# A selective-scan kernel: four states turned and three multiplied by GpSimd instead of three and four, their last columns kept by ScalarE, and the chunk loops written out

## The chip, the cores and the metric

One core of one Trainium2 chip. The metric is the device time of one execution in microseconds (us). The engines are TensorE (PE; PEld is its weight load), VectorE (DVE), ScalarE (ACT), GpSimd (POOL) and SyncE (SP), which here issues nearly all DMAs. Each engine runs its own list of instructions in order and waits on semaphores.

## The reference, cut to what matters

The input x is 2 x 4096 x 512. A layer norm with a modulation goes before two Mamba blocks, one forward and one backward in time; their outputs are projected, gated and added to x, and then a small quantized linear layer follows. The part that takes the time is the scan over 4096 positions, with 1024 channels and 16 states for each channel:

```
dA  = exp(delta[..., None] * A)
dBu = (delta * u)[..., None] * Bm[:, :, None, :]
def step(h, t):
    dA_t, dBu_t, C_t = t
    h = dA_t * h + dBu_t
    return (h, einsum('bdn,bn->bd', h, C_t))
y = (ys + u * Dp) * silu(z)
return y @ wout.T
```

## The kernel before, in words

There are three stages: a setup, the scan stage, which this change touches, and a final stage for the linear layer. The scan stage works through 32 chunks of 512 time steps (16 forward, 16 backward). A chunk has 8 tiles `j` of 128 channels, and a tile has 8 positions `q` of two states each, `n = 2q` and `2q + 1`; `p = 8j + q` counts the positions of a chunk, and `g` counts tiles over all chunks.

For every state of every tile:

- ACT computes dA = exp(delta * A) into one of four places (`step_dA`, L796 to L807; `PLACES = 4`). So dA of state n can be made only once state n - 4 no longer needs its place: for a straight state when DVE has multiplied it (`hC_made`), for the others when its scan is done (`h_made`).
- POOL computes dBu for two states at once (L692).
- DVE runs the scan h = dA * h + dBu (L1153).

Then the state is multiplied by C and summed over the 16 states. This is done in three ways:

- Nine straight states: DVE multiplies (L1169), and PE adds the product, transposed, into the bank `yT` (`add_state`, L1013 to L1018).
- `ASIDE`, four states (3, 4, 7, 11): the scan writes `hR`, POOL multiplies it in place (L701) at position `JOINS[n]`, three positions after the scan at most, and PE adds it there.
- `TURNED`, three states (1, 5, 9): the scan writes `hV`. PE transposes it into the one PSUM bank `OWN_BANK` (event `T`, `transpose_state`, L990) at position n // 2 + 1. ACT then takes it out at position `TAKE`, multiplying by C, which after the transpose is one number for each partition: four activations of 128 x 128 (`take_turned`, L769 to L775). At the start of the next tile PE adds these transposed pieces back (event `Y`, `turn_back`, L1020 to L1032), and DVE multiplies the result by the gate z (`gate`, L1121) at position 1.

The last column of each scan is the start of the same tile's scan in the next chunk. DVE copies it to `state`: straight states at L1165 and L1174, `hR` and `hV` states at L1183.

The rest of the network runs beside this as a background schedule (`SCHEDULE`): each event (Z and U: projections of four pairs of matmuls; O: output projection of eight; C: convolution; D: step; X, K, H: others) has positions at which PE issues its pieces, ahead of that position's additions to `yT`, and a `TAKE` position at which ACT empties its bank. A bank is written again only after it was taken (`bank_free`). Within a position PE goes by the first position of the event, and at equal first positions by Y, D, Z, T, others. So an O event that began earlier comes ahead of T.

Once a tile, at the positions in `GATED` (the last position of tiles 0 to 5 and 7, position 4 of tile 6), ACT loads the table for silu, runs one or two silus, and loads the table for exp again (L909 to L915). The order of ACT at a position is: dA of state 2q, then the `MIDWAY` takes (`Z` of this tile and the last `T` of a tile), dA of state 2q + 1, then the other takes, then the gated part. The lines that the steps of the prediction touch:

```
TAKE = {name: at[-1] + (2 if name[0] in "ZTUCDXK" else 1) ...}      # L101
PER_TILE += [(f"T{j*N+n}", (j*NQ + n//2 + 1,), OWN_BANK) ... for n in TURNED]   # L84
```

With TURNED = (1, 5, 9) the T events are at positions 1, 3 and 5 of a tile, and ACT takes them at 3, 5 and 7. The outer loops of ACT, PE, POOL and DVE are `Fori` loops of 4 rounds with 8 chunks written out in each.

Of the kernel before, what the change touches and what calls it, by code (L numbers as in the profile page):

```python
# [13 lines left out]
P = 128  # L14
D = 512
# [28 lines left out]
TURNED = (1, 5, 9)  # L44
ASIDE = (3, 4, 7, 11)
# [5 lines left out]
COPIES = ((3, 4), (7,), (11,))  # L51
# [3 lines left out]
HC, HR, HV = 4, 4, 3  # L55

TURN = 8
# [43 lines left out]
TAKE = {name: at[-1] + (2 if name[0] in "ZTUCDXK" else 1) for name, at, bank in SCHEDULE}  # L101
# [258 lines left out]
def scan_stage(nc, io, dram):  # L360

    with ExitStack() as ctx:
# [80 lines left out]
        def _(sp):  # L443
# [212 lines left out]
        def _(pool):  # L656
# [24 lines left out]
            with pool.Fori(0, CHUNKS // TURN) as r:  # L681
                for v in range(TURN):
                    i, s = r * TURN + v, v % 2
                    for j in range(MT):
                        g = i * MT + j
                        pool.wait_ge(du_made, g + 1)
                        for q in range(NQ):
                            p = j * NQ + q
                            pool.wait_ge(h_made, g * N + 2 * (q + 1 - AHEAD) + H0)
                            if j == 0:  # L690
                                pool.wait_ge(B_loaded[q], i * 16 + 16)
                            pool.tensor_tensor(dBu[:, q % AHEAD], Bb[:, 2 * q:2 * q + 2, :],  # L692
                                               du[:, j % 2, :].unsqueeze(1).broadcast_to([P, 2, T]),
                                               ALU.mult).then_inc(dBu_made, 1)
                            for n in ASIDE:
                                if q == JOINS[n]:
                                    k = ASIDE.index(n)
                                    pool.wait_ge(aside_saved, copied(g, n) + A0)
                                    if j == 0:
                                        pool.wait_ge(C_loaded[n // 2], i * 16 + 16)  # L700
                                    pool.tensor_tensor(hR[:, k, :], hR[:, k, :], Cb[:, n, :], ALU.mult).then_inc(hR_made, 1)  # L701
                            if q == 6:
                                m, ms = (j + 1, s) if j + 1 < MT else (0, 1 - s)
                                pool.wait_ge(dA_made, g * N + DU0)
                                pool.wait_ge(dBu_made, g * NQ + 1)
                                steps(g + 1, m, ms, i * MT + 2 * MT)

        @block.scalar
        def _(act):
            def take_step(made, bank, g, m):  # L710

                act.wait_ge(bg_ready, made)
                if not isinstance(g, int) or g > 0:
                    act.wait_ge(delta_made, g)
# [16 lines left out]
            def take_u(made, bank, c, m, stored):  # L731
                act.wait_ge(bg_ready, made)
                if m < 2 and not isinstance(c, int):
                    act.wait_ge(out_stored[m], c * 32 + O0)
                act.wait_ge(hist_stored, stored)
                if not isinstance(c, int) or m >= 2:
# [60 lines left out]
            def step_dA(g, j, v, n):  # L797
# [6 lines left out]
                else:  # L804
                    act.wait_ge(h_made, tile * N + before + 1 + H0)
                act.activation(place(n)[:], delta[:, j % 2, :], ACT.Exp,  # L806
                               scale=A[:, v % 2, j * N + n:j * N + n + 1]).then_inc(dA_made, 1)  # L807
# [36 lines left out]
            with act.Fori(0, CHUNKS // TURN) as r:  # L844
                for v in range(TURN):
                    i, s = r * TURN + v, v % 2
                    bank = lambda name: bg[BANK[name]]
                    act.wait_ge(bg_free, freed(i - 1, "K"))
                    act.wait_ge(A_loaded[s], r * (8 * TURN) + (v // 2 * 16 + 16))
# [778 lines left out]
```

## Time and profile before

| | |
|---|---|
| median of 3 runs | 7603.56 us (7603.14 to 7606.13) |
| profiled execution | 7600.66 us, of which the span is 7598.7 us |
| busy, share of the span | PE 90%, DVE 92%, POOL 92%, ACT 80% |
| granted TensorE clock, mean | 0.973 |
| costliest groups | POOL dBu (L692) 4788 us, DVE scans (L1153) 5165 us in three groups, ACT dA (L806) 2746 us, DVE products (L1169) 1557 us |

The first scan is at 225 us, the last at about 7160 us; nearly all of the rest is setup and final stage. How to read it: three engines are busy nine tenths of the span, so the shares alone don't say which one sets the time. The idle times ahead of each engine's instructions, and what ended them, do. A record of a DVE or ACT instruction reaches some 0.1 us into the next one's, so the time that an instruction really costs is the distance from its start to the next start.

### The profile page before, as it was taken

The page shows a single profiled execution, that of the slowest core. Times are in us where ns is not written, and L with a number is a line of the kernel's source. Part 1 is how long each engine was busy: PE and PEld are TensorE (multiplying, and loading weights), DVE is VectorE, ACT ScalarE, POOL GpSimd, SP SyncE. Part 2 cuts the span into 40 slices and gives each one's busy share as a digit, 9 for nine tenths or more (in the row PEclk, how much of TensorE's full clock was granted, in tenths as well). Part 3 has the DMA queues.
Part 4 walks back from the last instruction along what each step waited for, and adds up shares of the span by engine and source line. Part 5 has one row for each costly group of instructions (what it writes and reads, how often), then busy time and mean ns, then how long its engine had stood idle before and what let it go on. Part 6 is the DMA issues. An engine that isn't in the chain of part 4 may idle for free. (4 is left out here: it accounts for less than half of the span.)

```text
span 7598.7 us, 137446 instructions
## 1 busy us (share of the span) xinstructions
PE 6830.6 (90%) x32682; PEld 4035.6 (53%) x32682; DVE 6955.4 (92%) x10093; ACT 6069.6 (80%) x11545; POOL 6968.9 (92%) x3774
## 2 busy tenths in 40 slices
PE   6899999899898989999898999999898999999889
PEld 3455555555555555555555555555555555555455
DVE  2799999999999999999999999999999999999766
ACT  1788888888788888888788888888788888888645
POOL 0899999999999999999999999999999999999678
PEclk8999999999999999999999999999999999999999
DMA  8444445444444454444445544444355444444555
GB/s 258 145 137 134 128 139 149 128 120 144 132 134 126 141 150 124 123 143 138 122 129 145 149 113 136 139 137 134 117 150 149 107 141 135 138 130 131 152 193 172
DMA packets 605609, 1066.02 MB, mean 140 GB/s; under 512 B 113584, under 2 KB 221872, under 8 KB 596336
## 3 DMA queue, kind: packets, MB, share of 16 engines
q1 hardware_dynamic: 602704, 1055.84, 46.9%
q8 instruction: 289, 4.73, 0.3%
q14 instruction: 536, 4.39, 0.2%
q10 hardware_dynamic: 2080, 1.05, 0.0%
HBM read 926.61 MB, written 130.05 MB: 139 GB/s over the span
## 5 line engine op out<-in xcount | busy, mean ns | idle before, releaser
L692 POOL TENSOR_TENSOR dBu<-Bb,du 128x1024 f32<-128x1024 f32 x2048 | 4787.8, 2365 | 74.9 <-DVE hV L1153 44.2
L1153 DVE TENSOR_TENSOR_SCAN scans<-scans,state,dBu 128x512 f32<-128x512 f32 x2304 | 2902.8, 1280 | 393.6 <-ACT scans L806 363.1
L806 ACT ACTIVATE scans<-delta,A 128x512 f32<-128x512 f32 x4096 | 2745.7, 691 | 557.4 <-DVE hC L1169 480.9
L1016 PE MATMUL yT<-ident,hC 128*128 128x128 f32 x9216 | 1407.4, 282 | 344.1 <-DVE hC L1169 340.8
L1169 DVE TENSOR_TENSOR hC<-scans,Cb 128x512 f32<-128x512 f32 x2304 | 1556.8, 680 | 12.2 <-PE yT L1016 12.2
L1016 PEld LDWEIGHTS yT<-ident,hC 128*128 128x128 f32 x9216 | 1058.6, 143 | 774.8 <-DVE hC L1169 536.4
L701 POOL TENSOR_TENSOR hR<-hR,Cb 128x512 f32<-128x512 f32 x1024 | 1290.0, 1270 | 190.2 <-DVE state L1183 183.7
L1153 DVE TENSOR_TENSOR_SCAN hR<-scans,state,dBu 128x512 f32<-128x512 f32 x1024 | 1293.4, 1263 | 0.5
L1009 PE MATMUL bg<-u,comb 128*128 128x512 f32 x2112 | 989.1, 594 | 0.9 <-DVE u L1125 0.9
L1153 DVE TENSOR_TENSOR_SCAN hV<-scans,state,dBu 128x512 f32<-128x512 f32 x768 | 968.6, 1261 | 13.1 <-ACT scans L806 12.8
L948 PE MATMUL bg<-hT,win_u 128*128 128x512 f32 x2112 | 966.5, 598 | 0.9 <-ACT hT L728 0.9
L970 PE MATMUL bg<-hT,win_z 128*128 128x512 f32 x2048 | 963.3, 593 | 0.0
L773 ACT ACTIVATE turned<-bg,CT 128x128 f32<-128x128 f32 x3072 | 863.1, 363 | 14.4 <-PE bg L993 12.8
L1016 PEld LDWEIGHTS yT<-ident,hR 128*128 128x128 f32 x4096 | 493.1, 148 | 282.9 <-issue 254.7
L1016 PE MATMUL yT<-ident,hR 128*128 128x128 f32 x4096 | 620.9, 287 | 0.0
L948 PEld LDWEIGHTS bg<-hT,win_u 128*128 128x128 f32 x2112 | 382.3, 191 | 444.0 <-issue 437.7
L993 PEld LDWEIGHTS bg<-ident,hV 128*128 128x128 f32 x3072 | 369.2, 142 | 433.5 <-issue 257.6
L993 PE MATMUL bg<-ident,hV 128*128 128x128 f32 x3072 | 471.7, 276 | 90.0 <-ACT turned L773 59.8
L1009 PEld LDWEIGHTS bg<-u,comb 128*128 128x128 f32 x2112 | 368.6, 190 | 330.9 <-issue 329.2
L970 PEld LDWEIGHTS bg<-hT,win_z 128*128 128x128 f32 x2048 | 359.2, 190 | 306.0 <-issue 306.0
L963 PE MATMUL bg<-comb,wtap 128*32 128x512 f32 x2080 | 292.7, 636 | 212.1 <-DMA comb<-pre_scratch 207.1
L1027 PEld LDWEIGHTS bg<-ident,turned 128*128 128x128 f32 x3084 | 379.8, 149 | 155.5 <-issue 155.5
(163 smaller groups left out, 7586.9 us busy)
## 6 DMA issues: line engine op xcount, KB each, us to landing
comb<-pre_scratch SPq DMA_DIRECT2D x1040, 256.0 KB, 4.6
Bb<-bc_scratch SPq DMA_DIRECT2D x264, 512.0 KB, 8.6
Cb<-bc_scratch SPq DMA_DIRECT2D x264, 512.0 KB, 7.9
win_u<-in_win SPq DMA_DIRECT2D x264, 256.0 KB, 4.9
pre_scratch<-pre SPq DMA_DIRECT2D x264, 256.0 KB, 3.7
comb<-comb_scratch SPq DMA_DIRECT2D x66, 1024.0 KB, 8.0
win_z<-in_win SPq DMA_DIRECT2D x257, 256.0 KB, 2.7
part_scratch<-pre SPq DMA_DIRECT2D x132, 256.0 KB, 2.0
```

Source lines behind the costliest of these rows:

```text
L692: pool.tensor_tensor(dBu[:, q % AHEAD], Bb[:, 2 * q:2 * q + 2, :], du[:, j % 2, :].unsqueeze(1).broadcast_to([P, 2, T]), ALU.mult).then_in ...
L701: pool.tensor_tensor(hR[:, k, :], hR[:, k, :], Cb[:, n, :], ALU.mult).then_inc(hR_made, 1)
L773: ins = act.mul(turned[:, TURNED.index(n), tt * P:(tt + 1) * P], bank[:, tt * P:(tt + 1) * P], CT[:, s, tt, n:n + 1])
L806: act.activation(place(n)[:], delta[:, j % 2, :], ACT.Exp, scale=A[:, v % 2, j * N + n:j * N + n + 1]).then_inc(dA_made, 1)
L948: ins = nc.tensor.matmul(bank[:], win_u[:, m % RING, k, :], hT[:, slot, k, :], start=(k == 0), stop=(k == KD - 1))
L970: ins = nc.tensor.matmul(bank[:], win_z[:, j % 2, k, :], hT[:, slot, k, :], start=(k == 0), stop=(k == KD - 1))
L993: ins = nc.tensor.matmul(bank[:, tt * P:(tt + 1) * P], hV[:, TURNED.index(n), tt * P:(tt + 1) * P], ident[:], start=True, stop=True, is_tr ...
L1009: ins = nc.tensor.matmul(bank[:], comb[:, m, tt * P:(tt + 1) * P], u[:, s, m, :], start=(k == 0), stop=(k == MT - 1))
L1016: ins = nc.tensor.matmul(yT[:, tt * P:(tt + 1) * P], product[:, tt * P:(tt + 1) * P], ident[:], start=first and tt == 0, stop=False, is_tr ...
L1027: nc.tensor.matmul(bank[:, tt * P:(tt + 1) * P], turned[:, k, tt * P:(tt + 1) * P], ident[:], start=False, stop=False, is_transpose=True, ...
L1153: nc.vector.tensor_tensor_scan(to, place(n)[:], dBu[:, q % AHEAD, k, :], state[:, c:c + 1], ALU.mult, ALU.add).then_inc(h_made, 1)
L1169: nc.vector.tensor_tensor(hC[:, (j * NS + STRAIGHT.index(n)) % HC, :], bank[:], Cb[:, n, :], ALU.mult).then_inc(hC_made, 1)
```

## The change

1. `TURNED` becomes (2, 5, 8, 11) and `ASIDE` (1, 4, 7). The nine straight states are now 0, 3, 6, 9, 10, 12, 13, 14, 15. POOL multiplies three states a tile instead of four (at positions 3, 5 and 6); PE transposes four instead of three and adds four back.
2. T events are now at positions 2, 3, 5 and 6 of a tile, and ACT takes a turned state at the next position (3, 4, 6, 7), not at the one after that. The last of them is still taken midway in position 7.
3. The last columns of the turned and aside states are copied by ACT (`keep_states`), four positions of states later, not by DVE.
4. The `Fori` loops of ACT, PE, POOL and DVE are written out over all 32 chunks.
5. SP waits for `hR_used` (PE has added) instead of `hR_made` (POOL has multiplied) before it loads C again.

```
-TURNED = (1, 5, 9)
-ASIDE = (3, 4, 7, 11)
+TURNED = (2, 5, 8, 11)
+ASIDE = (1, 4, 7)
-COPIES = ((3, 4), (7,), (11,))
+COPIES = ((1,), (4,), (7,))
-HC, HR, HV = 4, 4, 3
+HC, HR, HV = 4, NA, NT
-TAKE = {name: at[-1] + (2 if name[0] in "ZTUCDXK" else 1) for name, at, bank in SCHEDULE}
+TAKE = {name: at[-1] + (2 if name[0] in "ZUCDXK" else 1) for name, at, bank in SCHEDULE}
...
-                            sp.wait_ge(hR_made, aside(last, 2 * q + 2))
+                            sp.wait_ge(hR_used, aside(last, 2 * q + 2) + R0)
...
-            with pool.Fori(0, CHUNKS // TURN) as r:
-                for v in range(TURN):
-                    i, s = r * TURN + v, v % 2
+            for i in range(CHUNKS):
+                s = i % 2
...
+            def keep_states(g, j, n):
+
+                for ns, places, saved in [(ns, hR, aside_saved) for ns in COPIES] + [(TURNED, hV, turned_saved)]:
+                    if n != ns[-1] + 4:
+                        continue
+                    act.wait_ge(h_made, g * N + ns[-1] + 1 + H0)
+                    k = (ASIDE if places is hR else TURNED).index(ns[0])
+                    step = ns[1] - ns[0] if len(ns) > 1 else 1
+                    act.copy(state[:, j * N + ns[0]:j * N + ns[-1] + 1:step],
+                             places[:, k:k + len(ns), T - 1]).then_inc(saved, 1)
...
+                        step_dA(g, i, j, 2 * q)
+                        keep_states(g, j, 2 * q)
...
+                        step_dA(g, i, j, 2 * q + 1)
+                        keep_states(g, j, 2 * q + 1)
...
-                            for n in pair:
-                                for ns, places, saved in [(ns, hR, aside_saved) for ns in COPIES] + [(TURNED, hV, turned_saved)]:
-                                    if n != ns[-1]:
-                                        continue
-                                    dve.wait_ge(h_made, g * N + n + 1 + H0)
-                                    k = (ASIDE if places is hR else TURNED).index(ns[0])
-                                    step = ns[1] - ns[0] if len(ns) > 1 else 1
-                                    nc.vector.tensor_copy(state[:, j * N + ns[0]:j * N + n + 1:step],
-                                                          places[:, k:k + len(ns), T - 1]).then_inc(saved, 1)
```

## Rows read from the trace of the kernel before

**Rows 1.** Waits over the whole span: who waited for whom, us in total, times, longest.

```profile
ACT scans L806 <- DVE hC L1169: 480.9, 465, 9.5
DVE scans L1153 <- ACT scans L806: 363.1, 195, 119.9
POOL hR L701 <- DVE state L1183: 183.7, 228, 1.5
DVE scans L1153 <- issue: 29.9, 3, 10.3
ACT turned L773 <- PE bg L993: 12.8, 30, 0.9
```

**Rows 2.** Groups of instructions by line and shape: busy us, mean ns of one, idle before.

```profile
L701 POOL TENSOR_TENSOR hR<-hR,Cb 128x512 f32<-128x512 f32 x1024 | 1290.0, 1270 | 190.2 <-DVE state L1183 183.7
L1183 DVE COPY state<-hV 128x3 f32<-128x3 f32 x256 | 89.5, 350 | 0.0
L1183 DVE COPY state<-hR 128x2 f32<-128x2 f32 x256 | 79.2, 309 | 0.0
L1183 DVE COPY state<-hR 128x1 f32<-128x1 f32 x512 | 73.6, 144 | 0.0
L874 ACT ACTIVATE state<-state,cur 128x16 f32<-128x16 f32 x256 | 75.6, 295 | 0.0
```

**Rows 3.** Busy time by tile of chunk 12: window, length, PE, PEld, DVE, ACT, POOL, clock, DMA.

```profile
2852.90:2879.90 27.00, 27.00 (x127) 16.59 (x128) 26.30 (x38) 20.64 (x40) 26.82 (x16) 1.00 0.10 33
...
sum 214.46, PE 196.48 PEld 116.96 DVE 207.68 ACT 182.00 POOL 208.25; mean PE 24.56 PEld 14.62 DVE 25.96 ACT 22.75 POOL 26.03
```

**Rows 4.** Timeline of PE in tile 1 (2852.90 to 2879.90): start us, us, instruction.

```profile
2861.06 0.60 PE L1016 MATMUL yT<-ident,hC 128*128 128x128 f32 x4
2861.49 1.88 PE L1009 MATMUL bg<-u,comb 128*128 128x512 f32 x4
2863.21 1.88 PE L970 MATMUL bg<-hT,win_z 128*128 128x512 f32 x4
2864.93 0.60 PE L993 MATMUL bg<-ident,hV 128*128 128x128 f32 x4
...
2872.71 0.60 PE L1016 MATMUL yT<-ident,hC 128*128 128x128 f32 x4
```

**Rows 5.** Timeline of ACT in the same tile.

```profile
2861.40 1.12 ACT L773 ACTIVATE turned<-bg,CT 128x128 f32<-128x128 f32 x4
...
2875.14 0.78 ACT L782 ACTIVATE pre<-bg,gain 128x512 f32<-128x512 f32 x1 [0.87 <-PE bg L1009]
2875.94 1.28 ACT L909 ACT_TABLE_LOAD   x1
...
2879.18 1.91 ACT L806 ACTIVATE scans<-delta,A 128x512 f32<-128x512 f32 x3
```

**Rows 6.** Timeline of DVE in the same tile: scans of states 6, 8, and the next tile.

```profile
2861.89 0.85 DVE L1183 COPY state<-hR 128x2 f32<-128x2 f32 x1
2862.65 1.28 DVE L1153 TENSOR_TENSOR_SCAN scans<-scans,state,dBu 128x512 f32<-128x512 f32 x1
...
2865.67 0.14 DVE L1183 COPY state<-hR 128x1 f32<-128x1 f32 x1
2865.73 1.28 DVE L1153 TENSOR_TENSOR_SCAN scans<-scans,state,dBu 128x512 f32<-128x512 f32 x1
...
2879.90 1.29 DVE L1153 TENSOR_TENSOR_SCAN scans<-scans,state,dBu 128x512 f32<-128x512 f32 x1 [0.71 <-ACT scans L806]
```

**Rows 7.** Timeline of PE and ACT at the end of tile 3 (2906.56 to 2933.04).

```profile
2925.09 0.60 PE L993 MATMUL bg<-ident,hV 128*128 128x128 f32 x4
...
2926.40 0.60 PE L1016 MATMUL yT<-ident,hC 128*128 128x128 f32 x4
...
2928.13 1.28 ACT L909 ACT_TABLE_LOAD   x1
...
2932.31 1.92 ACT L806 ACTIVATE scans<-delta,A 128x512 f32<-128x512 f32 x3
```

More of the change, by code:

```diff
@@ L712, in take_step @@
                 act.wait_ge(bg_ready, made)
-                if not isinstance(g, int) or g > 0:
+                if g > 0:
                     act.wait_ge(delta_made, g)
@@ L944, in project_u @@
                 pe.wait_ge(wu_loaded[m % RING], (c * per + m // RING + 1) * 16)
-                if m == 0 and not isinstance(c, int):
+                if m == 0 and c > 0:
                     pe.wait_ge(bg_free, freed(c - 2, "H3"))
@@ new lines, in _ @@
+            for i in range(CHUNKS):
+                s = i % 2
+                for j in range(MT):
+                    g = i * MT + j
+                    dve.wait_ge(state_kept, g - 6 + K0)
+                    for q in range(NQ):
+                        p = j * NQ + q
+                        dve.wait_ge(state_saved, kept(g, q) + S0)
+                        dve.wait_ge(dBu_made, g * NQ + q + 1)
+                        for k in range(2):
+                            n = 2 * q + k
+                            c = j * N + n
+                            dve.wait_ge(dA_made, g * N + n + 1 + DU0)
+                            if n in ASIDE:
+                                dve.wait_ge(hR_used, aside(g, n) + 1)
+                                to = hR[:, ASIDE.index(n), :]
+                            elif n in TURNED:
+                                dve.wait_ge(bg_ready, ready(i if j else i - 1, f"T{((j - 1) % MT) * N + n}"))
+                                dve.wait_ge(turned_saved, g + V0)
+                                to = hV[:, TURNED.index(n), :]
+                            else:
+                                to = place(n)[:]
+                            nc.vector.tensor_tensor_scan(to, place(n)[:], dBu[:, q % AHEAD, k, :],
+                                                         state[:, c:c + 1], ALU.mult, ALU.add).then_inc(h_made, 1)
+                        if q == 1:
+                            name = f"Y{(j - 1) % MT}"
+                            gate(ready(i, name), bg[OWN_BANK], g - 1, (j - 1) % MT, s if j else 1 - s)
+                        pair = (2 * q, 2 * q + 1)
+                        own = [n for n in pair if n in STRAIGHT]
+                        for n in own:
+                            c = j * N + n
+                            dve.wait_ge(h_made, g * N + n + 1 + H0)
+                            bank = place(n)
+                            if len(own) == 1:
+                                nc.vector.tensor_copy(state[:, c:c + 1], bank[:, T - 1:T]).then_inc(state_saved, 1)
+                            dve.wait_ge(hC_used, straight(g, n) - C0 + 1)
+                            if j == 0 and n == own[0]:
+                                dve.wait_ge(C_loaded[q], i * 16 + 16)
+                            nc.vector.tensor_tensor(hC[:, (j * NS + STRAIGHT.index(n)) % HC, :], bank[:],
+                                                    Cb[:, n, :], ALU.mult).then_inc(hC_made, 1)
+                            if n == pair[0]:
+                                dve.wait_ge(h_made, g * N + n + 2 + H0)
+                            if n == pair[0] and len(own) == 2:
+                                nc.vector.tensor_copy(state[:, c:c + 2],
+                                                      scans[:, n % PLACES:n % PLACES + 2, T - 1]).then_inc(state_saved, 1)
```

275 lines of the change are left out of this document (112 added, 163 removed).

## The prediction

> **What bounds the kernel now.** I read the waits first, then the groups of instructions, then one chunk tile by tile, and last the timeline of two tiles.
>
> The busy shares name three candidates, POOL, DVE and PE, each near nine tenths. The waits separate them [rows 1]. DVE's scans wait for dA of ACT: 363.1 us in total, of which 119.9 us is the one wait ahead of the first scan, so about 243 us fall within the scan stage. DVE has no wait of this size for POOL. POOL in turn waits 183.7 us for DVE's copies. So POOL, though as busy as DVE, is not what the scans wait for. ACT is the least busy of the four, but it works in order and waits 480.9 us for DVE's products, because it has only four places for dA. The picture: DVE sets the pace, and where ACT is held up in one place for long, DVE stops.
>
> Rows 3 show it for chunk 12, 214.46 us long: DVE is busy 207.68 us of it, POOL 208.25, PE 196.48, ACT 182.00. In tile 1 PE is busy 27.00 us of 27.00: there PE has no slack at all. Most tiles end with a stop of DVE for dA of the next tile's first state, as at 2879.90, 0.71 us [rows 6]: just before, ACT did its two table loads and silu.
>
> **What goes away.**
>
> POOL's fourth multiply: 256 x 1.27 us = 325 us of POOL's busy time [rows 2]. I count it at nothing, since no scan waits for POOL [rows 1]. At most it could be worth what POOL costs elsewhere.
>
> By the Trainium skill, GPSIMD Engine Reference, sections 1 (Specifications) and 2 (Architecture), GpSimd shares its SBUF port with VectorE, which contends with it in instructions with two SBUF inputs. If DVE stood still for all of the removed 325 us, the time would be 7603.6 - 325 = 7279. The trace speaks against it: DVE's scans take 1.28 to 1.29 us wherever they stand beside POOL's work [rows 6].
>
> DVE's copies for `hR` and `hV`: four a tile. Their busy times sum to 89.5 + 79.2 + 73.6 = 242 us [rows 2], but records overlap. From start to next start the one-column copy costs 0.06 us (2865.67 to 2865.73) and the slow two-column one 0.76 us (2861.89 to 2862.65) [rows 6]. Bounds: 256 x 4 x 0.06 = 61 us, and 242 us. I take about 90 us of DVE time. It is worth that only in tiles where DVE itself is the last; where DVE waits for ACT it is worth nothing.
>
> The loops: three waits of about 10 us, 29.9 us in all, that no engine ended [rows 1]; they are the three jumps back of the four-round loops. Written out they go: -30 us. The other waits are then on constants instead of registers. What a hand-over costs is seen at 2879.18: dA of 0.65 us, and the scan that waits for it starts at 2879.90 [rows 5, 6], so at most 0.1 us could go. Two such hand-overs a tile would be 51 us; I count 0 and keep the 51 us of gain as the bound.
>
> **What is added.** ACT gets four more activations a tile for the fourth turned state. Four of them cost 1.0 us from the first to the next instruction's start (the block of 1.12 us includes the tail) [rows 5], so 256 us. It also gets four small copies a tile; the nearest row is its 128x16 multiply, 295 ns [rows 2], whose real cost lies between 0.1 and 0.3 us; 0.2 x 4 x 256 = 205 us. PE gets one transpose group and one turn-back group more, one addition less: +4 matmuls of 128x128 a tile at 0.44 us a group [rows 4]. ACT's 182 us a chunk become about 196 of 214: it still fits on average. Averages don't decide here; order does.
>
> **The order.** Before, a turned state had two positions between PE's transpose and ACT's take, and ACT waited only 12.8 us in all for it [rows 1]. A position lasts 3.1 us or more (2862.65 to 2865.73) [rows 6]. Now it has one position. ACT reaches the take one position (over 3 us) earlier, while PE's transpose of the same position comes no earlier. So ACT will wait, and what stands behind the take on ACT is dA of states 2q + 2 and on, and at a tile's end the table loads, silu, and dA of the next tile's first state. DVE waits for those. I work out two tiles.
>
> Tile 1, middle. Now the second turned state (2) is transposed at position 2. PE's addition for position 1 stood at 2861.06; it moves up 0.44 us, as T of position 1 is gone, and ends about 2861.06. Ahead of T at position 2 come the two pieces of O1 (1.72 us) and of Z1 (1.72 us), then T with its tail, 0.60: ready at 2865.1 [rows 4]. ACT began its take in the same position 3 at 2861.40 [rows 5]; now it begins at 2865.1, ends it 1.0 us later, and makes dA of state 8 in 0.65: 2866.8, where DVE wants it at 2865.73 [rows 6]. DVE stops for 1.1 us.
>
> Tile 1, end. PE's own chain: T of position 3 waits for the bank until 2866.2, 1.3 us later than its 2864.93; the turn-back has 0.44 more. So the addition of state 10 moves from 2872.71 to about 2874.4 and ends at 2874.9. At position 6 the two O2 pieces come first (1.72), then the new T of state 11: ready about 2877.1. ACT takes it midway in position 7: 1.0, then dA of state 15, 0.65, the copy of four columns, 0.2, O2's take, 0.8: 2879.75. From the table load to dA of the next tile it is 3.24 us (2875.94 to 2879.18), and that dA takes 0.7 [rows 5]: the next tile starts at 2883.7, not 2879.90, less the 0.1 us by which PE's chain closes up: +3.7 us.
>
> Tile 3, end (no O pieces at position 6). PE's addition of state 10 ends about 2926.4, and T of state 11 is ready at 2927.0 [rows 7]. But ACT must first take state 8 (transposed at position 5, where a transpose stood at 2925.09: ready at 2925.7), 1.0, then dA of state 14, 0.65: 2927.35. Take, dA 15, copy and U3's take (as O2's): 1.0 + 0.65 + 0.2 + 0.8: 2930.0. Table load to dA is 4.18 us here, with two silus (2928.13 to 2932.31), plus 0.7: 2934.9 against 2933.04, +1.8 us.
>
> The other tiles by the same steps in the same views, by what stands ahead of T: tile 2 has O3 and Z2 pieces ahead of T of state 2 and U0, U1 (3.4 us each) at positions 4 and 5: +3.8. Tile 5 has the convolution C6 at position 5, which waits for a DMA: +3.8. Tile 6 has its table loads at position 4, and the take of state 5 now stands ahead of them with its 1.0 us, after a late one of state 2: +2.6. Tile 4 has U4 at position 1: +1.6; tile 7 +1.4; tile 0, with the least ahead of T, +0.9. These are estimates of mine from the timelines of PE and ACT, of which rows 4, 5 and 7 stand for two tiles.
>
> **The sum.** A chunk: 0.9 + 3.7 + 3.8 + 1.8 + 1.6 + 3.8 + 2.6 + 1.4 = 19.6 us, 9% of 214.46. Times 32: +627 us. The copies taken from DVE give nothing in it, as every tile now ends with a wait for ACT. Loops: -30. Profiled execution 7600.7 + 627 - 30 = 8198; the median lies 3 above the profiled one: 8200 us, rounded.
>
> Other places: SP now waits for PE's addition before it reloads C, so the loads of B behind it in SP's queue come later by a few us once a chunk. POOL needs B of the next chunk two positions or more later, and chunks get longer: 0, with 2 us x 32 = 64 as the bound above.
>
> **Rivals.**
>
> 1. Less of it. Only the tile ends count, and PE is never behind. Then state 11's T comes right after the addition of state 10, as in tile 3, and the middle of tiles costs nothing: 6 to 12 us a chunk. 7600.7 - 30 + 192 to 384 = 7760 to 7955. For it: ACT has up to three states of lead, and a longer tile gives PE time to catch up. Against: PE is full in tile 1 [rows 3], and what stands ahead of T is PE's own work.
>
> 2. Faster. T is ready when ACT comes, so the order costs nothing, and DVE's copies and the loops are gained: 7603.6 - 30 - 61 = 7512, down to 7603.6 - 30 - 242 = 7332 by the busy times. It decides at one point: whether PE has T of state 11 ready when ACT has made dA of state 14. For it: ACT is idle a fifth of a chunk [rows 3]. Against: that idle time is waiting for DVE's products [rows 1], and the table loads come after the take.
>
> 3. POOL runs dry. POOL's multiply of state 4 at position 5 now waits for ACT's copy, which comes behind dA of state 8; in tile 1 that is 2867.0, and POOL still has multiplies of 1.23 each, dBu of 2.3 each and the steps, about 10.7 us, before dBu of the last position, which the scan wants at 2876.7. It is late by 1 us there, in the three heavy tiles: 3 x 32 x 1.1 = +106 us, 8306, and more only if POOL's lateness carried from tile to tile.
>
> 4. No change: rival 1's lower half meets rival 2's gains, 7590 to 7615.
>
> **How the numbers follow.** The forecast (8000 to 8400: a third of the 627 less, or rival 3 and the 64 us of the loads more) has 0.55, rival 1 0.27, rival 2 0.10, the port rule 0.01, rival 4 0.04, rival 3 above 8400 0.03. Likeliest: 8200 us. The range reaches from 7680 to 8400: below it are the cases of faster and no change (0.15), above it 0.03. A measurement of this kernel tells 0.2% (15 us) from no change. Faster 0.11, within 0.2% 0.04, slower 0.85.
>
> **What would show each step.** ACT's turned group waits for PE's transposes by hundreds of us instead of 12.8. DVE's scans wait for ACT's dA by over 700 us instead of 243 in the stage, at a tile's first state and at state 8. The wait "issue" of 29.9 us is gone. POOL's busy time falls by about 325 us and its idle time grows by more. Tiles 1, 2 and 5 are over 30 us long. The prediction is wrong if ACT's takes find T ready as before, or if the scans' waits for ACT don't grow.

## The result and the profile after

The median is 8305.32 us (8303.13 to 8310.12, 4 runs) against 7603.35 us for the kernel before in the same set: the ratio is 1.0925, interval 1.0911 to 1.0939, so 702 us slower. The profiled execution took 8304.09 us, its span is 8302.3 us and the mean granted clock 0.958, against 0.973.

Part 1 of the page of the kernel after (busy us, share of the span, instructions):

```profile
PE 7105.6 (86%) x33710; PEld 4219.8 (51%) x33710; DVE 6887.6 (83%) x9069; ACT 6412.4 (77%) x13593; POOL 6662.7 (80%) x3518
```

No engine is above 86% now. GpSimd, relieved of a quarter of its multiplies, and VectorE, relieved of its copies, both stand idle a sixth of the time or more. Where they stand is in the waits. These are the waits of the kernel after that answer to [rows 1] (who waited for whom, us in total, times, longest):

```profile
POOL hR L698 <- ACT state L814: 1270.1, 639, 6.7
ACT turned L770 <- PE bg L1002: 966.7, 576, 4.7
DVE scans L1160 <- ACT scans L803: 888.8, 479, 119.9
DVE hV L1160 <- PE bg L1002: 179.9, 128, 2.4
PE bg L1002 <- ACT turned L770: 162.0, 192, 1.2
ACT scans L803 <- DVE hC L1176: 82.0, 128, 1.3
DVE hV L1160 <- ACT scans L803: 74.3, 93, 1.6
DVE scans L1160 <- issue: 24.9, 124, 0.2
```

ACT's take waits 966.7 us for PE's transpose, where it waited 12.8 us before. The scans wait 888.8 us for dA; less the 119.9 us ahead of the first scan that is 769 us, against 243. Another 254 us are lost ahead of the scans that write `hV`, all of them at state 8. Summed by state over the 256 tiles, without the wait ahead of the very first scan, the scans' stops are 443 us at state 0, 254 at state 8, 178 at state 10, 144 at state 15 and 31 at state 14; in the kernel before they are 178 (30 of them the jumps of the loops), 16, 79, 0 and 0. ACT's waits for VectorE's products have shrunk from 480.9 to 82.0 us: ACT no longer runs ahead of VectorE, it runs behind. The three waits of 10 us are gone (no "issue" wait of a scan is over 0.2 us).

Three groups of the kernel after, to be set beside [rows 2] (busy us, mean ns | idle before):

```profile
L698 POOL TENSOR_TENSOR hR<-hR,Cb 128x512 f32<-128x512 f32 x768 | 977.6, 1273 | 1270.5 <-ACT state L814 1270.1
L770 ACT ACTIVATE turned<-bg,CT 128x128 f32<-128x128 f32 x4096 | 1175.7, 380 | 975.4 <-PE bg L1002 966.7
L814 ACT COPY state<-hR 128x1 f32<-128x1 f32 x768 | 155.4, 202 | 0.0
```

Chunk 12 by tile, the windows of the kernel after, from first scan to first scan (columns as in [rows 3]):

```profile
3093.23:3120.88 27.65, 27.01 (x118) 15.73 (x117) 25.86 (x33) 22.09 (x48) 24.79 (x14) 0.95 0.56 222
3120.88:3151.44 30.56, 29.08 (x139) 17.84 (x138) 25.68 (x34) 22.74 (x49) 27.05 (x15) 1.00 0.09 29
3151.44:3181.74 30.30, 27.77 (x130) 16.71 (x128) 25.86 (x34) 23.14 (x52) 24.52 (x14) 1.00 0.46 126
3181.74:3211.00 29.26, 25.88 (x141) 14.76 (x140) 25.64 (x33) 24.65 (x54) 25.28 (x14) 1.00 0.55 137
3211.00:3239.63 28.63, 23.93 (x121) 13.32 (x119) 25.56 (x34) 24.73 (x54) 23.26 (x14) 1.00 0.61 148
3239.63:3270.66 31.03, 26.39 (x145) 16.14 (x143) 25.67 (x34) 25.26 (x55) 27.78 (x15) 1.00 0.45 106
3270.66:3304.48 33.82, 23.32 (x97) 11.65 (x96) 25.77 (x33) 26.89 (x55) 22.88 (x13) 0.89 0.18 53
3304.48:3332.04 27.56, 22.20 (x123) 16.73 (x122) 25.64 (x35) 23.26 (x51) 23.12 (x14) 0.87 0.58 186
```

VectorE is busy about 25.7 us in every tile, however long the tile is: all that was added is standing still. The chunk is 238.8 us long against 214.46 [rows 3]. The lengths of the same tiles of the kernel before, from first scan to first scan, give the growth:

| tile | 0 | 1 | 2 | 3 | 4 | 5 | 6 | 7 |
|---|---|---|---|---|---|---|---|---|
| before, us | 26.3 | 27.0 | 26.7 | 26.5 | 26.8 | 27.7 | 28.1 | 25.5 |
| after, us | 27.7 | 30.6 | 30.3 | 29.3 | 28.6 | 31.0 | 33.8 | 27.6 |
| growth | 1.4 | 3.6 | 3.6 | 2.8 | 1.8 | 3.4 | 5.8 | 2.1 |
| growth, mean of all chunks | 1.5 | 3.5 | 3.6 | 2.5 | 1.8 | 2.8 | 5.4 | 1.8 |
| forecast | 0.9 | 3.7 | 3.8 | 1.8 | 1.6 | 3.8 | 2.6 | 1.4 |

The fourth line is the same difference in the mean of the 32 chunks, without the three jumps. Chunk 12 is not typical in one tile: before the change its tile 5 took 27.7 us, where the mean of that tile is 29.0.

### The profile page after: what moved, and what is told of

It is laid out like the page before. It is cut to its first block and busy times, and to the rows that moved or that the text cites. A ratio compares the mean times of both kernels' runs of the same rounds, so it can differ in the third digit from the quotient of the medians.

```text
span 8302.3 us, 112807 instructions
## 1 busy us (share of the span) xinstructions
PE 7105.6 (86%) x33710; PEld 4219.8 (51%) x33710; DVE 6887.6 (83%) x9069; ACT 6412.4 (77%) x13593; POOL 6662.7 (80%) x3518
## 5 line engine op out<-in xcount | busy, mean ns | idle before, releaser
L1160 DVE TENSOR_TENSOR_SCAN scans<-scans,state,dBu 128x512 f32<-128x512 f32 x2304 | 2908.9, 1278 | 923.0 <-ACT scans L803 888.8
L698 POOL TENSOR_TENSOR hR<-hR,Cb 128x512 f32<-128x512 f32 x768 | 977.6, 1273 | 1270.5 <-ACT state L814 1270.1
L770 ACT ACTIVATE turned<-bg,CT 128x128 f32<-128x128 f32 x4096 | 1175.7, 380 | 975.4 <-PE bg L1002 966.7
L1160 DVE TENSOR_TENSOR_SCAN hV<-scans,state,dBu 128x512 f32<-128x512 f32 x1024 | 1298.8, 1268 | 254.3 <-PE bg L1002 179.9
L1160 DVE TENSOR_TENSOR_SCAN hR<-scans,state,dBu 128x512 f32<-128x512 f32 x768 | 970.6, 1264 | 0.0
L1002 PE MATMUL bg<-ident,hV 128*128 128x128 f32 x4096 | 651.1, 283 | 162.0 <-ACT turned L770 162.0
L1002 PEld LDWEIGHTS bg<-ident,hV 128*128 128x128 f32 x4096 | 496.1, 144 | 561.3 <-issue 315.3
L1036 PEld LDWEIGHTS bg<-ident,turned 128*128 128x128 f32 x4112 | 501.8, 149 | 183.1 <-issue 183.1
L1036 PE MATMUL bg<-ident,turned 128*128 128x128 f32 x4112 | 519.9, 282 | 0.0
L1025 PE MATMUL yT<-ident,hR 128*128 128x128 f32 x3072 | 481.0, 280 | 0.0
L1025 PEld LDWEIGHTS yT<-ident,hR 128*128 128x128 f32 x3072 | 374.5, 146 | 149.1 <-issue 149.1
```

Source lines behind the costliest of these rows:

```text
L770: ins = act.mul(turned[:, TURNED.index(n), tt * P:(tt + 1) * P], bank[:, tt * P:(tt + 1) * P], CT[:, s, tt, n:n + 1])
L1002: ins = nc.tensor.matmul(bank[:, tt * P:(tt + 1) * P], hV[:, TURNED.index(n), tt * P:(tt + 1) * P], ident[:], start=True, stop=True, is_tr ...
L1025: ins = nc.tensor.matmul(yT[:, tt * P:(tt + 1) * P], product[:, tt * P:(tt + 1) * P], ident[:], start=first and tt == 0, stop=False, is_tr ...
L1036: nc.tensor.matmul(bank[:, tt * P:(tt + 1) * P], turned[:, k, tt * P:(tt + 1) * P], ident[:], start=False, stop=False, is_transpose=True, ...
L1160: nc.vector.tensor_tensor_scan(to, place(n)[:], dBu[:, q % AHEAD, k, :], state[:, c:c + 1], ALU.mult, ALU.add).then_inc(h_made, 1)
```

## Inside two tiles

**Tile 1**, for which the prediction worked out every step. From the timelines of PE, ACT and DVE of the kernel after, put in order of time (start us, us, instruction, in brackets the idle time before it):

```profile
3132.39 0.60 PE L1002 MATMUL bg<-ident,hV 128*128 128x128 f32 x4
3133.02 1.14 ACT L770 ACTIVATE turned<-bg,CT 128x128 f32<-128x128 f32 x4 [1.38 <-PE bg L1002]
3134.04 0.71 ACT L803 ACTIVATE scans<-delta,A 128x512 f32<-128x512 f32 x1
3135.04 1.28 DVE L1160 TENSOR_TENSOR_SCAN hV<-scans,state,dBu 128x512 f32<-128x512 f32 x1 [2.08 <-PE bg L1002]
...
3144.21 0.60 PE L1002 MATMUL bg<-ident,hV 128*128 128x128 f32 x4
3144.84 1.14 ACT L770 ACTIVATE turned<-bg,CT 128x128 f32<-128x128 f32 x4 [1.31 <-PE bg L1002]
...
3151.44 1.29 DVE L1160 TENSOR_TENSOR_SCAN scans<-scans,state,dBu 128x512 f32<-128x512 f32 x1 [2.30 <-ACT scans L803]
```

The tile starts at 3120.88. The transpose of state 2 is ready 12.1 us into it (forecast 2865.1 - 2852.90 = 12.2), the one of state 11 at 23.9 (forecast 24.2), and the tile is 3.6 us longer (forecast 3.7). The stop in the middle is 2.08 us, where 1.1 was forecast. The scan of state 8 starts 14.2 us into the tile (forecast 13.9), so most of the difference seems to be on the other side: VectorE had done its product 12.1 us into the tile and not 12.8, as the slow two-column copy of [rows 6] is no longer ahead of it. What the copy gave back is stood still here, one instruction on. (The profile names PE as the releaser, since this scan waits for several semaphores; the transpose in question is that of the tile before and was long done. Of what the scan needs, dA came last: it was begun at 3134.04, behind the take, and ended 0.29 us before the scan; dBu had ended 5 us before it.)

**Tile 6**, where the forecast was worst. The timelines of PE and DVE of the kernel after, in order of time:

```profile
3286.90 1.93 PE L988 MATMUL bg<-u,wx 128*64 128x512 f32 x4
3288.76 0.65 PE L1002 MATMUL bg<-ident,hV 128*128 128x128 f32 x4
...
3291.31 1.29 DVE L1160 TENSOR_TENSOR_SCAN scans<-scans,state,dBu 128x512 f32<-128x512 f32 x1 [5.05 <-ACT scans L803]
...
3294.47 1.11 PE L1025 MATMUL yT<-ident,hC 128*128 128x128 f32 x4 [4.62 <-DVE hC L1176]
3295.51 3.68 PE L988 MATMUL bg<-u,wx 128*64 128x512 f32 x4
3299.12 1.12 PE L1002 MATMUL bg<-ident,hV 128*128 128x128 f32 x4
...
3302.03 1.29 DVE L1160 TENSOR_TENSOR_SCAN scans<-scans,state,dBu 128x512 f32<-128x512 f32 x1 [2.53 <-ACT scans L803]
```

And the windows of the same stretch (the number ahead of the DMA share is the granted clock):

```profile
3285.00:3290.00 5.00, 3.82 (x19) 1.78 (x17) 1.23 (x3) 4.95 (x8) 1.47 (x1) 1.00 0.00 0
3290.00:3292.50 2.50, 0.00 (x0) 0.00 (x0) 1.19 (x1) 2.49 (x6) 0.52 (x1) 1.00 0.00 0
...
3295.00:3297.50 2.50, 2.50 (x6) 0.92 (x5) 2.50 (x5) 0.64 (x2) 2.50 (x2) 0.50 0.00 0
3297.50:3300.00 2.50, 2.50 (x6) 0.89 (x6) 1.82 (x2) 0.00 (x0) 2.50 (x2) 0.50 0.04 7
```

The first stop, at state 10, is the one that was forecast: ACT does its table loads and silus at position 4, now with the take of state 5 ahead of them. It is 5.05 us, where the kernel before stopped 2.44 us: 2.6 us more, exactly the term of the sum. What the sum did not have is the second stop, 2.53 us at state 15. While VectorE stood, PE had nothing to add and was idle for 4.62 us, and then its granted clock fell from 1.00 to 0.50, the lower of its two levels (1.2 GHz). The piece of the projection X that stands ahead of the transpose of state 11 took 3.68 us; the same four matmuls took 1.93 us at 3286.90. In another chunk of the same execution the piece took 2.84 us (PE and DVE of its tile 6):

```profile
4971.23 2.84 PE L988 MATMUL bg<-u,wx 128*64 128x512 f32 x4
4976.45 1.29 DVE L1160 TENSOR_TENSOR_SCAN scans<-scans,state,dBu 128x512 f32<-128x512 f32 x1 [1.24 <-ACT scans L803]
```

There, in chunk 19, the stop at state 15 is 1.24 us, not 2.53, and the tile 32.5 us long, not 33.8: of 32 chunks 18 have the long form of 33.8 us, and the others lie between. In all 32 the stop at state 10 is followed by a stretch at the clock of 0.50. From the start of the X piece to ACT's take it is 4.77 us in chunk 12 (3295.51 to 3300.28), and 2.51 us at full clock (3286.90 to 3289.41, the end of the transpose behind it). So the clock costs up to 2.3 us a chunk, at most 2.3 x 32 = 74 us in all. That is an estimate from these rows; no run kept the clock up. The Trainium skill, TensorE: Matmul & The Clock Gate, Part 1, has an idle TensorE fall to half its clock; the trace agrees.

## The experiments

The theory: ACT's takes wait for PE's transposes, and all that stands behind a take on ACT, dA above all, comes late to VectorE. Runs 1 to 4, runs 5 to 8 and runs 9 to 12 are three sets, each taken on another chip with the kernel before beside it; the medians of the kernel before are 7617.0, 7600.9 and 7604.4 us. A ratio is always to the kernel before of the same set. Two runs of one set can be compared in us; two runs of different sets are compared by their ratios, times 7603 us.

**1. The loops alone.** The kernel before, with only its four loops written out:

```
-            with pool.Fori(0, CHUNKS // TURN) as r:
-                for v in range(TURN):
-                    i, s = r * TURN + v, v % 2
+            for i in range(CHUNKS):
+                s = i % 2
```

> The kernel before with only its four outer loops written out over the 32 chunks; states, takes and copies as before. My theory: only the three jumps back go, 30 us: 7573 us, ratio 0.996. Rival (waits on registers cost time at each hand-over): up to 50 us more, 7520 us.

7574.66 us, ratio 0.9943 (0.9927 to 0.9960): 42 us (30 to 56) less than the kernel before beside it. That 7574.66 is 29 us below the 7603.35 of the section above is no measure, as that is another set. 30 us are the three jumps, which are gone from the waits; whether the other 12 us are a gain on constants instead of registers, the runs don't tell.

**2. Takes one position on, nothing else.** Run 1 with its sets of states kept, (1, 5, 9) turned:

```
-TAKE = {name: at[-1] + (2 if name[0] in "ZTUCDXK" else 1) for name, at, bank in SCHEDULE}
+TAKE = {name: at[-1] + (2 if name[0] in "ZUCDXK" else 1) for name, at, bank in SCHEDULE}
```

> The same as the first, and one thing more: the three turned states (1, 5, 9) are taken by ACT one position after PE's transpose (positions 2, 4, 6) instead of two. No work is added. Order theory: ACT comes ahead of PE and waits, and dA behind it is late: 3 to 8 us a chunk more than the first run, 7670 to 7830 us, with ACT's wait for PE's transposes at hundreds of us. Rival (what costs in the change is ACT's added work, not the order): as the first run, 7573 us.

7842.06 us, ratio 1.0295 (1.0277 to 1.0312): 12 us above the range expected, and 267 us over run 1, for one character of the code and no work added. Its waits:

```profile
ACT turned L770 <- PE bg L990: 807.7, 490, 3.4
DVE scans L1148 <- ACT scans L803: 359.2, 348, 4.4
```

The stops ahead of the scans sum to 454 us in its scan stage, against 249 in run 1: 205 of the 267 us. (The profile puts 78 us of them, at state 10, down to GpSimd's dBu; that dBu had ended 6 us or more before these scans, and what came last is again dA.) Some 44 us more are on another path, VectorE's copies of last columns. The rows of run 1 and of run 2:

```profile
L1178 DVE COPY state<-hV 128x3 f32<-128x3 f32 x256 | 99.3, 388 | 0.0
L1178 DVE COPY state<-hV 128x3 f32<-128x3 f32 x256 | 160.0, 625 | 0.0
```

The three-column copy got 61 us longer in all, the two-column one 17 us shorter (run 8 shows what such copies wait for). So not all of the 267 us is the wait that run 2 was made to show.

**3. The last turned state late, nothing else.** Run 1 with state 11 as the last turned one (transposed at position 6, taken midway in position 7), the others taken two positions on, three turned and four aside as before (the line of `TAKE` gets a condition for it, and `COPIES` follows `ASIDE`):

```
-TURNED = (1, 5, 9)
-ASIDE = (3, 4, 7, 11)
+TURNED = (1, 6, 11)
+ASIDE = (3, 4, 7, 9)
```

> The kernel before with loops written out and the turned states 1, 6, 11 (multiplied by GpSimd: 3, 4, 7, 9), so the amount of work of every engine is that of before; states 1 and 6 are taken two positions after their transpose, state 11 (transposed at position 6) midway in position 7, where state 9 (transposed at position 5) was taken. Order theory, tile ends alone: 6 to 12 us a chunk more than the first run, 7760 to 7955 us. Rival (added work costs): 7573 us, within 15.

7952.30 us, ratio 1.0442 (1.0425 to 1.0460): 378 us over run 1, again for the same work. The scans' wait for dA is now the large one, 342 us at state 0 (148 in run 1) and 205 at state 15 (none in run 1):

```profile
DVE scans L1149 <- ACT scans L804: 623.7, 319, 6.6
```

So both places of the forecast exist, the takes in the middle of a tile and the late one at its end. Rival 1, only the tile ends, had the price of its own part right (192 to 384 us) and missed the other 267. The two, the loops and run 11 below (55 us over run 1 by the ratios) add up to -42 + 267 + 378 + 55 = 658 us of the 702. That the parts may be added was not tested: runs 2 and 3 both shorten the slack of the last turned state. The 44 left are for the fourth turned state and for what the parts do to each other, which was not tried apart.

**4. GpSimd relieved.** The kernel before, with GpSimd's multiply of state 4 cut to 32 columns:

```
-    pool.tensor_tensor(hR[:, k, :], hR[:, k, :], Cb[:, n, :], ALU.mult).then_inc(hR_made, 1)
+    w = 32 if n == 4 else T
+    pool.tensor_tensor(hR[:, k, :w], hR[:, k, :w], Cb[:, n, :w], ALU.mult).then_inc(hR_made, 1)
```

> The kernel before, where GpSimd multiplies only 32 of the 512 columns of state 4 (so the sum over states is changed for the other columns, and 480 columns of work are left out in each of 256 tiles): GpSimd is relieved by about what the change takes from it. My theory: no scan waits for GpSimd, so 7603 us, within 15. Rival (GpSimd sets the pace, or its work slows VectorE through a shared port): down to 7603 - 300 = 7300 us.

7611.87 us, ratio 0.9995 (0.9986 to 1.0005). Nothing, as forecast, with GpSimd busy 6715.3 us instead of 6968.9. Only GpSimd's own waits grew, from the 183.7 us of [rows 1] to

```profile
POOL hR L702 <- DVE state L1184: 412.0, 354, 3.2
```

**5. Transposes first.** The kernel after; at each position PE now issues the transpose ahead of the other pieces:

```
-                for name, at, own in SCHEDULE:
+                for name, at, own in sorted(SCHEDULE, key=lambda entry: entry[0][0] != "T"):
```

The list `BY_END`, by which the events are counted, is sorted to match.

> The changed kernel, where PE does the transposes of turned states ahead of all other background pieces of their position; nothing else is changed. Order theory: in tiles 0 to 4, 6 and 7 the transpose of state 2 had 1.7 to 3.5 us of projection pieces ahead of it, and in tiles 1 and 6 that of state 11 had pieces of O2 and X; VectorE's stops at state 8 (273 us in the changed kernel) mostly go, and some 2 us each of the ends of tiles 1 and 6: 7900 to 8050 us. Rival (ScalarE's added work is what costs, wherever PE puts the transposes): 8290 us or more.

7952.54 us, ratio 1.0459 (1.0441 to 1.0477): some 353 us less than after, half of what the change costs, with the same work. ACT's wait for the transposes is halved:

```profile
ACT turned L770 <- PE bg L1002: 465.0, 448, 4.5
DVE scans L1160 <- ACT scans L803: 791.8, 354, 121.0
```

The forecast had the pieces of O, Z, U and X ahead of the transposes as the reason. For the half that went this is shown: the stops at state 8 fall from 254 to 35 us. The stops at state 0 stay, 430 us against 443, so the pieces ahead of the last transpose are not what holds up the tile ends.

**6. The turned states earlier.** The kernel after with (3, 5, 7, 9) turned and (1, 4, 11) aside, so that the last transpose is at position 5 and no take stands at a tile's end:

```
-TURNED = (2, 5, 8, 11)
-ASIDE = (1, 4, 7)
+TURNED = (3, 5, 7, 9)
+ASIDE = (1, 4, 11)
```

`COPIES` follows `ASIDE`.

> The changed kernel with the turned states 3, 5, 7, 9 and the aside states 1, 4, 11: the same amount of work on every engine, four turned and three aside; the transposes are at positions 2 to 5, the takes at 3, 4, 5 and midway in 6, so none stands ahead of the table loads at a tile's end. Order theory: the tile ends are as in the first run (e1_loops), the middles cost as in e2_take1 (267 us over e1_loops) or somewhat more, as there are four: 7850 to 7980 us. Rival (added work costs): 8305 us, within 30.

8321.84 us, ratio 1.0940 (1.0921 to 1.0958). The expectation was wrong by over 340 us. The waits point to the reason:

```profile
DVE scans L1160 <- ACT scans L803: 1220.7, 793, 121.0
ACT turned L770 <- PE bg L1002: 782.7, 576, 5.0
PE bg L1002 <- ACT turned L770: 461.4, 352, 4.5
```

The transposes now stand at four positions in a row, and all go through one bank. The stops at the tile ends did shrink (state 0 from 443 to 144 us, state 15 from 144 to none), but those at states 12 and 13 came to 396 us, and the ones at state 8 grew from 254 to 340. PE waits for ACT's take (461.4 us, in the kernel after 162.0) before it can write the next transpose, and then ACT waits for PE in turn. The stops moved into the tiles. That the one bank is the cause is read from these waits and was not tested.

**7. Both.** Run 6 with the transposes first, as in run 5.

> e6_early and e5_turned_first together. Order theory: 7650 to 7800 us, near the kernel before, with all the work of the change in it. Rival (added work): 8290 us.

7875.23 us, ratio 1.0359 (1.0341 to 1.0376): 447 us less than run 6, by the order of issue alone, and 75 us above the expectation. Of its waits, ACT for PE is 295.7 us and PE for ACT 290.7; the one bank may be what is left. Of the four kernels with the work of the change (after, 5, 6 and 7) the slowest and the fastest are 447 us apart. The fastest of them, this one, is by the ratios still 316 us over run 1, which turns three states; how much of that is the added work and how much the bank is open. Banks of their own for the turned states were not tried: `scans` holds four banks, `bg` three and `yT` one.

**8. The copies back on VectorE.** The kernel after with `keep_states` taken out and the old copies put back at VectorE's place, the turned states' as one copy of four columns.

> The changed kernel with the copies of last columns given back to VectorE (where the kernel before had them); takes, states and loops as changed. GpSimd's 1270 us of waiting for ScalarE's copies go to VectorE's earlier copies. My theory: these waits cost nothing, as GpSimd's last dBu of a tile is only 0.1 us ahead of where the scan wants it and the tile's end is set by ScalarE; ScalarE's chain gets 0.2 us a tile shorter (-50 us), VectorE's longer: 8240 to 8310 us. Rival (GpSimd ran dry for the late copies, my third rival): 8200 us or less.

8403.29 us, ratio 1.1036 (1.1009 to 1.1064): 98 us slower than after by the medians (84 by the ratios), and 93 above the range that was expected. The groups of its copies by shape, and the timeline around one of them:

```profile
L1178 DVE COPY state<-hV 128x4 f32<-128x4 f32 x256 | 344.8, 1347 | 0.0
L1178 DVE COPY state<-hR 128x1 f32<-128x1 f32 x768 | 104.4, 136 | 0.0
L1169 DVE COPY state<-scans 128x2 f32<-128x2 f32 x512 | 71.5, 140 | 0.0
```

```profile
3101.43 2.35 POOL L689 TENSOR_TENSOR dBu<-Bb,du 128x1024 f32<-128x1024 f32 x1 [1.99 <-DVE hV L1148]
3101.91 1.89 DVE L1178 COPY state<-hV 128x4 f32<-128x4 f32 x1
```

A copy of four columns, 16 bytes a partition, lasts 1.89 us. It ends at 3103.80, and GpSimd's instruction ended at 3103.78. That is no chance: 252 of the 256 copies are longer than 0.25 us, and all of these end 23 to 33 ns after the end of the GpSimd instruction that was in progress; beside the other four that instruction had less than 0.25 us to go. The one-column copies (136 ns) never do this, nor do the two-column copies out of `scans`, which lies in PSUM (140 ns; 510 of 512 began while GpSimd worked). The two-column and three-column copies out of `hR` and `hV` in [rows 2] (309 and 350 ns) are the same thing in small: the 61 and 69 of them that are longer than 0.25 us end 23 to 31 ns after GpSimd's instruction, and the others are short because GpSimd was idle or had less than 0.25 us to go. ACT's copy of the same four columns out of `hV` in the kernel after does not wait: 205 to 318 ns.

**9. One column at a time.** Run 8 with the copy split:

```
-nc.vector.tensor_copy(state[:, j * N + ns[0]:j * N + n + 1:step],
-                      places[:, k:k + len(ns), T - 1]).then_inc(saved, 1)
+for m in ns:
+    k = (ASIDE if places is hR else TURNED).index(m)
+    ins = nc.vector.tensor_copy(state[:, j * N + m:j * N + m + 1], places[:, k, T - 1:T])
+ins.then_inc(saved, 1)
```

> As e8_copies_vector, but the last columns of the four turned states are copied by four VectorE copies of one column each, not by one strided copy of four columns. In e8 the strided copy took 1347 ns on average and up to 2359, ending with GpSimd's instruction, the one-column copies 136 ns. Theory now: VectorE's copies of more than one column wait for GpSimd's instruction to end, and that, 256 x 1.3 = 300 us less what was hidden, made e8 slow; without it my expectation for e8 holds: 8150 to 8310 us. If ScalarE's late copies cost GpSimd and so the time (third rival), it comes below 8150 us. Rival (the copies' place on VectorE costs in itself): as e8, 8400 us.

8285.42 us, ratio 1.0893 (1.0875 to 1.0911): 118 us less than run 8 by the medians (109 by the ratios) for three instructions more a tile. All 1024 one-column copies out of `hV` began while GpSimd worked, and none took over 0.15 us. The time is also 20 us less than after (24 by the ratios), with intervals that touch. So whether ACT or VectorE copies matters little in this schedule, but not because nothing changed: the scans' stops shrink from 1055 to 941 us, and VectorE's own time between them grows by about as much, 96 us. Run 9 alone therefore doesn't decide rival 3, that GpSimd runs dry because its multiplies wait for ACT's copies. The trace of the kernel after does: only at state 14 does dBu come last, ahead of 156 of 256 scans, and these stops sum to 31 us (the row "issue" of 24.9 us above and 7.0 put down to dBu). In run 9 they are 0.1 us.

**10. The same in the kernel before.** Run 1 (the kernel before, loops written out) with one-column copies.

> As e1_loops (three turned states, two positions, written-out loops), but with VectorE's last-column copies one column each: five of 50 ns more instead of one of three and one of two columns, which averaged 388 and 310 ns. Theory: 0 to 60 us less than e1_loops, 7515 to 7575 us; where ScalarE holds VectorE up anyway, nothing is gained. Rival (several columns at once cost no more): e1_loops plus 10 us.

7547.02 us (7542.3 to 7552.2), ratio 0.9923 (0.9906 to 0.9939): the lowest ratio of all, about 760 us less than the change. Over run 1 it gains 28 us by the medians, but they are of different sets; by the ratios it is 15 us, and the intervals overlap, so a gain is not shown. In the traces VectorE's time between stops is 47 us shorter than in run 1 and its stops are 19 us longer.

**11. The third part of the change alone.** Run 1 with the copies on ACT four states later, and SP's later wait (the fifth part).

> As e1_loops, with the last columns of turned and aside states copied by ScalarE as in the change (three copies for aside states and one for turned ones a tile) and SyncE's later wait: the third part of the change alone. Order theory: VectorE gains 0.2 to 0.5 us a tile, ScalarE's chain at a tile's end (table loads) gets up to 0.2 us longer: between 50 us less and 60 us more than e1_loops, 7520 to 7630 us. Rival (the copies carry a good part of the change's loss): above 7650 us.

7616.21 us, ratio 1.0015 (1.0003 to 1.0028): 55 us over run 1 by the ratios (42 by the medians), and 69 over run 10 of the same set. VectorE is relieved of its copies and yet loses. Two of its waits:

```profile
POOL hR L698 <- ACT state L814: 284.0, 212, 4.7
...
DVE scans L1160 <- issue: 158.6, 194, 1.7
```

GpSimd waits longer for ACT's late copies than it did for VectorE's (188.5 us in run 1), and the scans now stop for 158.6 us with no releaser named, where run 1 has no such wait. All of them are at state 14 (159 us summed over its 256 scans), and in seven of the eight tiles that scan starts 0.09 us after the end of GpSimd's dBu for it, in the median of the chunks. So GpSimd does become late in a tight schedule: here rival 3's mechanism is seen in the trace.

**12. Transposes first in the kernel before.** Run 10 with the edit of run 5.

> As e10_loops_single, with PE's transposes of turned states ahead of the other pieces of their position. With two positions between transpose and take, ScalarE hardly waits for them (12.8 us in the kernel before), so there is little to gain; PE may stand at the transpose of state 5 until ScalarE has taken state 1. Order theory: within 40 us of e10. If it gains, it is the fastest so far.

7862.50 us, ratio 1.0336 (1.0318 to 1.0353): 315 us over run 10, the opposite of run 5, where at most 40 were expected. Two waits of PE in run 12:

```profile
PE bg L990 <- DVE u L1121: 284.4, 207, 2.2
PE bg L990 <- ACT turned L770: 118.5, 50, 3.7
```

With the transposes at the head of the queue, PE comes to them before their bank is free (VectorE's `gate` and ACT's take empty it), and the pieces of the projections, which would have filled the time, stand behind. With two positions to the take, as here, hardly anyone had waited for the transpose (12.8 us [rows 1]), so there was nothing to win.

## Why the prediction was right, and where it was off

The forecast was 8200 us, the result 8305: slower, by the mechanism named, and inside the range. The range of 7680 to 8400 is wide and holds rival 1 too; what speaks for the mechanism are runs 2, 3 and 5 and the tiles. That rival 3's 8306 us is the number measured is chance: its mechanism cost 31 us and not the 106 that were added for it.

- **What bounds the kernel.** Right. GpSimd's busy time fell by 306 us (forecast 325), and such relief was worth nothing (run 4: 0.9995 for 254 us of its multiplies), and the order on ACT was worth hundreds of us with no work added (runs 2 and 3).
- **The port rule as rival.** For the scans it is dead, but the scans are no test of its condition: they read one large operand from SBUF and one from PSUM. Where both ends are in SBUF, in the small copies, the contention is there (run 8). The Trainium skill says as much: GPSIMD Engine Reference, section 1 (Specifications), names contention with VectorE's "2-port" mode, and VectorE: DVE Perf Modes, section "Mode 2×_2P", gives that mode to copies within SBUF and not to PSUM sources. The prediction left the 2-port mode out and held the rule against the wrong instructions.
- **VectorE's copies.** The price of 90 us was a mean over two kinds that should have been kept apart. Their waits were seen (0.85 us for two columns [rows 6]) and not explained. What splitting them is worth where VectorE sets the pace is within the noise (run 10: 15 us by the ratios). "Nothing in the sum" for their removal was about right: run 9 against after is 20 us the other way. The reason given, that every tile now ends with a wait for ACT, was not: tile 7 starts without one, as before the change.
- **The loops.** -30 forecast, -42 (-30 to -56) measured beside the kernel before; the jumps alone are 30.
- **ACT's added work.** The takes cost 1.02 us from start to start (3133.02 to 3134.04), forecast 1.0. The copies were priced at 0.2 us each; from start to start one costs 0.09 (3146.47 to 3146.56, record 0.21). That is some 110 us of ACT's time too much, hidden by the next point.
- **The order, tile by tile.** In chunk 12 tiles 1, 2, 4 and 5 were within 0.4 us, their misses and those of tile 0 (+0.5) and tile 7 (+0.7) come to +0.6 together. Tile 3 was 1.0 short, tile 6 3.2. That makes the 4.8 us by which chunk 12 grew more than forecast (24.4 against 19.6). In the mean of all chunks tile 5 was 1.0 too dear, which makes up for what was missing in tiles 0 and 7: that part of the closeness is luck. Of the places of the stops the forecast named states 0 and 8, and in tile 6 the one behind the table loads (state 10); the 144 us at state 15 were not foreseen.
- **The term that was mis-sized: tile 6.** 2.6 forecast, 5.8 measured. The stop at state 10 was right to 0.1 us; the second stop, at state 15, 2.53 us in chunk 12 and 1.24 in the shortest case, was not in the sum. Up to 2.3 us of it is the price that the first stop has for PE, the clock at 0.50 while the next transpose is due. Tile 6 is two thirds of what chunk 12 is over its forecast, and 2.8 of 3.2 us in the mean of the chunks.
- **The sum.** 19.6 us a chunk against (702 + 30) / 32 = 22.9 in the mean of all chunks; 3.3 x 32 = 105 us is the distance from 8200 to 8305.
- **Rival 1** had half of the mechanism (runs 2 and 3). **Rival 2** failed at its point of decision: ACT waits for the transpose of state 11 by 1.31 us in tile 1. **Rival 3** has 31 us in the kernel after, where it said 106; in the tighter schedule of run 11 the same mechanism stops the scans for 159 us, and the kernel is 55 us slower.
- **The 64 us for SP's later wait** were rightly left at 0: GpSimd's dBu waits 3.2 us in all for B.

## What to carry to other kernels

Between in-order engines that hand a buffer round, ask for each hand-over how many us lie between the producer's place and the consumer's, and what stands behind the consumer. One position taken from that slack cost 267 us here (205 of them in stops of the scans), and placing the last hand-over a position later 378, while 254 us of work taken from an engine that was 92% busy were worth nothing. Moving a piece to the head of a queue helps only if someone waits for it and its buffer is free by then: the same edit gave 353 us in one schedule and cost 315 in the other.

## What the runs showed of the hardware

- A VectorE copy from SBUF to SBUF of two to four columns waits until the GpSimd instruction in progress has ended: up to 2.36 us, 1.35 us in the mean of the four-column ones, for 16 bytes a partition. With one column, or out of PSUM, it takes 0.14 us. That the count of columns decides is shown for the four columns by run 9, where 1024 one-column copies out of the same tile ran beside GpSimd's work without waiting; for two and three columns, and for the kind of source, it was seen in the groups. ACT's copies don't wait so. The reason inside the engine is only argued.
- A stop of 4.6 us of TensorE in the middle of a kernel that keeps it 86% busy was followed in all 32 chunks by a granted clock of 0.50 (in chunk 12 from 3295 to 3300), just when the work that had piled up is due.
- Three jumps back of loops whose bodies are eight chunks long stopped the scans for 10 us each (29.9 us in all [rows 1]).
